# Deviations of sequences 8 to 15 in one batch, the query shift ahead of VectorE's extra work, and column sums of the second weight in step 14

## The reference

```python
x = x + tanh(g_xattn[0]) * xattn(layernorm(x), ctx, ctx, Wq, Wk, Wv, Wo)
x = x + tanh(g_ffn[0]) * ffn(layernorm(x), w1, conv_w, conv_b, w2)

def xattn(q, k, v, ...):            # 16 heads of 16 features
    probs = softmax((q @ Wq.T) @ (k @ Wk.T).T / sqrt(16))
    return (probs @ (v @ Wv.T)) @ Wo.T

def ffn(x, w1, conv_w, conv_b, w2): # 256 -> 1024 -> 256
    h = act_quant(x) @ weight_quant(w1).T     # 8 bit by token, ternary by weight
    h = silu(depthwise_conv1d(h, conv_w, conv_b))   # 3 taps along the sequence
    return act_quant(h) @ weight_quant(w2).T
```

## Time and profile before

| | |
|---|---|
| median of 3 runs | 218.56 us (218.4 to 218.66) |
| the profiled execution | 218.36 us, of which 216.6 are its span |
| busy share of the span | TensorE 92%, its weight loads 75%, VectorE 83%, ScalarE 73%, GpSimd 68% |
| chain of work that ended last | GpSimd 42%, issue 22%, TensorE 18%, VectorE 12% |
| granted TensorE clock, mean | 0.992 of full speed |

### The profile page before, as it was taken

One profiled execution on the slowest core, in us unless ns is written; L12 is line 12 of the kernel. 1 busy time (PEld: TensorE's weight loads), 2 busy tenths in 40 slices (PEclk: granted clock), 3 DMA queues, 4 the chain that ended last, 5 costly groups with the idle time before them and its releaser, 6 DMA issues.

```text
span 216.6 us, 6146 instructions
## 1 busy us (share of the span) xinstructions
PE 199.2 (92%) x2267; PEld 162.9 (75%) x2267; DVE 179.2 (83%) x384; ACT 157.9 (73%) x273; POOL 147.2 (68%) x219
## 2 busy tenths in 40 slices
PE   6999899999989999999979999999989939899995
PEld 6988778788777878788767878877758717687784
DVE  4358686988989898898969889898899979998982
ACT  2347575685866879898878989987989936876541
POOL 2630411853527567988898698898878898999971
PEclk9999999999999999999999999999999988999999
DMA  5999101113022120212210210000002223546543
GB/s 159 338 354 319 51 26 52 47 50 79 20 69 53 38 86 16 73 27 62 53 36 16 55 33 17 2 12 3 3 0 48 51 48 94 101 102 166 116 133 122
DMA packets 29120, 16.95 MB, mean 78 GB/s; under 512 B 17546, under 2 KB 28834, under 8 KB 29090
## 3 DMA queue, kind: packets, MB, share of 16 engines
q1 hardware_dynamic: 29090, 16.55, 28.1%
HBM read 10.50 MB, written 2.11 MB: 58 GB/s over the span
## 4 chain that ended last, share of the span: by engine, by line
POOL 42%; issue 22%; PE 18%; DVE 12%; ACT 2%; DMA 1%; POOLq 1%; DVEq 0%; ACTq 0%
POOL y L489 10%; POOL hid L470 4%; POOL xT L433 4%; POOL xT L435 4%; POOL w2f L477 4%; POOL rstd L442 3%; POOL xn L454 3%; PE ps_av L572 3%; POOL var L439 3%; PE ps_score L657 2%; POOL xq L462 2%; DVE zmax L1438 2%; DVE y L1310 2%; PE ps_proj L623 2%; PE ps_max L667 2%
## 5 line engine op out<-in xcount | busy, mean ns | idle before, releaser
L1253 DVE TENSOR_REDUCE smax<-ps_max 128x8 f32<-128x1024 f32 x31 | 37.8, 1221 | 15.0 <-PE ps_max L667 12.6
L1010 ACT ACTIVATE prob<-ps_score 128x1024 f32<-128x1024 f32 x32 | 32.7, 1020 | 11.5 <-PE ps_score L657 10.6
L657 PE MATMUL ps_score<-Qs,KT 32*128 32x128 f32 x512 | 37.1, 282 | 2.6 <-DVE Qs L1261 1.4
L489 POOL TENSOR_TENSOR y<-y,tap 128x508 f32<-128x508 f32 x30 | 38.6, 1289 | 0.9 <-DVE y L1310 0.6
L657 PEld LDWEIGHTS ps_score<-Qs,KT 32*128 32x128 f32 x512 | 31.2, 186 | 10.0 <-issue 3.7
L667 PE MATMUL ps_max<-KT,QT 32*128 32x256 f32 x248 | 35.1, 400 | 0.0
L454 POOL TENSOR_SCALAR xn<-xn,qa 128x256 f32<-128x256 f32 x16 | 8.6, 536 | 23.2 <-DVE qa L1293 23.1
L1310 DVE SCALAR_TENSOR_TENSOR y<-hid,conv,y 128x508 f32<-128x508 f32 x24 | 23.3, 973 | 0.8 <-ACT y L1048 0.8
L667 PEld LDWEIGHTS ps_max<-KT,QT 32*128 32x128 f32 x248 | 21.1, 184 | 0.1
L477 POOL TENSOR_SCALAR w2f<-y,zmax 128x1024 f16<-128x1024 f32 x16 | 18.0, 1122 | 2.3 <-DVE zmax L1443 1.0
L1438 DVE TENSOR_REDUCE zmax<-y 128x1 f32<-128x1024 f32 x16 | 19.3, 1207 | 0.0
(11 more groups left out here) (145 smaller groups left out, 500.2 us busy)
## 6 DMA issues: line engine op xcount, KB each, us to landing
cin<-ctxT SPq DMA_DIRECT2D x16, 128.0 KB, 3.1
xres<-x SPq DMA_DIRECT2D x16, 128.0 KB, 5.5
out<-xres SPq DMA_DIRECT2D x16, 128.0 KB, 2.0
xT<-xT SPq DMA_DIRECT2D x12, 128.0 KB, 2.3
norm_bc<-norm_dram SPq DMA_DIRECT2D x12, 128.0 KB, 3.2
w1f<-w1T SPq DMA_DIRECT2D x1, 1024.0 KB, 7.3
w2f<-w2T SPq DMA_DIRECT2D x1, 1024.0 KB, 8.7
wk<-wkT SPq DMA_DIRECT2D x1, 256.0 KB, 2.8
```

The lines of the kernel that those rows point to most:

```text
L489: gp.tensor_tensor(y3[:, :, 0:P - 1], y3[:, :, 0:P - 1], tap_buffer(T), ALU.add).then_inc(conv_gp, 1)
L657: mm = pe.matmul(ps_score[:, i * 512 + j * P:i * 512 + (j + 1) * P], KT[b % 3][rows, j * P:(j + 1) * P], Qs[rows, j * P:(j + 1) * P], star ...
L1010: act.activation(prob[pair][:, :], ps_score[:, :], ACT.Exp, scale=DH ** -0.5).then_inc(exp_done, 1)
L1253: dve.tensor_reduce(dst, first_max(n, pair)[:, :].rearrange("p (g t e k) -> p g t e k", g=PG, t=KD, e=2), AX.X, ALU.max).then_inc(max_done, 1)
```

## The change

The statistics of sequences 12 to 15 are taken in step 2 as well, so that GpSimd makes the deviations of sequences 8 to 15 in one batch of eight; the batch of sequences 14 and 15 with its rows, its write and its step is gone. On VectorE shift_q moves ahead of the first slot for extra work, in all steps. The column sums and their copy move from step 7 to step 14, into the PSUM of the values (`ps_v`), in place of the matrices that kept TensorE busy; the first transposes of the last group of quantised inputs now wait for that copy.

```diff
-SUMS_STEP = SB + 3
...
-ROWS = {2: (4, 8), 4: (8, 14), 11: (14, 16)}
+ROWS = {2: (4, 8), 4: (8, 16)}
...
-        ps_w2sum = ps_h[:, 0:D]
+        ps_w2sum = ps_v
...
                 if n == 8:
-                    write_rows(8, 14, 2)
-                if n == 15:
-                    write_rows(14, NB, 3)
-                    load_rows(14, 3)
+                    write_rows(8, NB, 2)
                 turn_xq(n - 6)
-                if n != 14:
-                    load_rows(n, 2 if n < 14 else 3)
+                load_rows(n, 2)
...
                 if s == 2:
-                    norm_rows(8, 14, 4)
-                if s == 9:
-                    norm_rows(14, NB, 5)
+                    norm_rows(8, NB, 4)
...
                 if d >= LAST:

-                    pe.wait_ge(v_done, NB)
+                    pe.wait_ge(sum2_done, 1)
...
-                if d == SUMS_STEP - 3:
-                    pe.wait_ge(sum2_done, 1)
...
-                pe.wait_ge(xq_done, 2 * SB)
-                pe.wait_ge(raw_done, gp_tiles(TILES[SUMS_STEP][0]))
-                pe.wait_ge(scaled_dve, dve_tiles(TILES[SUMS_STEP][0]))
+                pe.wait_ge(k_done, NB)
+                pe.wait_ge(v_done, NB)
...
-                if s == SUMS_STEP:
-                    w2_column_sums()
-                elif seq(d - 1):
+                if seq(d - 1):
                     int_transpose(d - 1, min(tiles, default=0))
                 if seq(n):
                     project_q(n)
-                if s == SUMS_STEP:
-                    int_transpose(d - 1, min(tiles))
...
                 if seq(n + 1):
                     project_k(n + 1)
                 else:
-                    pe.wait_ge(v_done, NB)
-                    keep_busy(4, ps_k)
+                    w2_column_sums()
...
-                if s == SUMS_STEP:
-                    w2_sums_copy()
...
                     k_copy(n + 1)
+                else:
+                    w2_sums_copy()
...
+                shift_q(b)
                 extra(0)
-                shift_q(b)
...
                 if k == 0:
-                    stats_of(10, 11)
+                    stats_of(10, 11, 12)
                 else:
                     weight_scale(0)
-                    stats_of(12, 13)
+                    stats_of(13, 14, 15)
...
-            step(SB + 3, lambda k: stats_of(14) if k == 1 else None)
-            step(SB + 4, lambda k: stats_of(15) if k == 1 else None)
-            for s in range(SB + 5, NB - 1):
+            for s in range(SB + 3, NB - 1):
                 step(s)
```

## The result

The changed kernel takes 215.89 us (median of 4 runs, 215.48 to 216.37) against 218.55 for the kernel before on the same chip (4 runs, 218.4 to 218.66): ratio 0.9881, 95% interval 0.9869 to 0.9894, 2.66 us faster.

The account below looks back on a forecast made before the run. TensorE bounds an ordinary step at a pace of 9.1 us, GpSimd close behind. The terms -0.1 (steps 2 to 6), -0.2 (step 7), -1.3 (step 10) and -0.45 (step 11) sum to -2.05: forecast 216.5 us, range 215.3 to 217.9.

Parts of the forecast that it names:

- Steps 10 and 11: End of the batch: both steps fall to the 9.1 pace without the small batch and its rows, gaining 1.3 and 0.45.
- Column sums: Moved from step 7 to 14: only 0.2 of TensorE's 1.03 arrives; bounds 0 and 1.03.
- Rival 1: Column sums' whole 1.03 arrives, as step 7's GpSimd chain moves forward with an earlier row_max: 215.7; chance 0.12.
- The start of the batch: Steps 1 to 3: two more sequences on VectorE and GpSimd's eight-wide norm_rows cost 0.5, bounds 0.3 and 0.9.
- both delays meet: VectorE's 0.3 and GpSimd's 0.53 meet at the same row stage, so the later counts: 0.5, not their sum.
- The power's 0.53 for two more elements: GpSimd's norm_rows at the batch's start: 1.60 for six is 0.27 each, so two more cost 0.53.
- The shift: Steps 3 to 6, shift_q ahead of extra work: 0.6 gained, limited by VectorE's 0.65 idle in step 5; bounds 0, 1.2.
- go into the lateness above: Step 3: the 0.53 wait for Qs goes into the lateness from the batch's start, not counted as shift gain.
- Rival 4: Normalise behind the weight passes makes TensorE about 0.6 late in each of steps 3 to 6: slower, 219.5; chance 0.10.
- Contention: GpSimd's norm2 power, 0.80 beside weight passes in step 4 and 0.58 in step 3, may take 0.2 more in step 3.
- In step 3 ScalarE's wait for GpSimd: Sign named for the batch's start: a longer wait than the 1.46 ScalarE already stood for norm2's result.
- Everything from step 12 on: Every engine starts the same work earlier by the same amount, so the gain of 2.05 carries to the end.

Follow-up runs that it names:

- the kernels that each removed one of them: Changed kernel with two of step 2's deviations ahead of shift_q: 215.79 us; changed kernel with GpSimd's batch behind norm2 of step 3: 215.86 us.
- the shift alone: Kernel before with only shift_q moved ahead of VectorE's extra work: 217.31 us against 218.58, ratio 0.9937.
- batch alone: Kernel before with only the deviations of sequences 8 to 15 made in one batch: 217.67 us against 218.58, ratio 0.995.
- two deviations ahead and the batch moved: Changed kernel with two deviations ahead of shift_q in step 2 and GpSimd's batch behind norm2 of step 3: 215.58 us against 218.51, ratio 0.9867.
- the last piece apart: Changed kernel with the second weight's last piece split, one pass in step 6, one each ending steps 7 and 9: 215.67 us against 218.51, ratio 0.987.

## Why the prediction was right, and where its sum was off

**Steps 10 and 11** were right in size and mechanism: 1.77 measured for 1.75, ScalarE's wait for GpSimd in step 10 down from 1.71 to 0.31, no wait of project_q in step 11.

**Column sums**: 0.2 forecast; 0.07 to 0.23 by the marks and 0.18 by the times beside the batch, about 0.35 alone. The reason held as well: raw sets step 7. Rival 1's 215.7 lies nearer to the measured 215.89 than the forecast's 216.5, and it is false; only the kernels without the other parts could show that.

**The start of the batch**: 0.5 forecast, 0.42 measured with the shift. That both delays meet and only the later one counts was right, and the kernels that each removed one of them show it: neither gained, both together gained 0.49. Against the shift without a batch (58.81), VectorE's delay alone costs 0.36, where 0.3 was forecast. The power's 0.53 for two more elements was wrong: it divided the whole instruction by six. Where no weight pass runs beside it, the power takes 1.05 for four elements, 1.36 for six (the shift alone) and 1.67 for eight, 0.16 for each further one, 0.31 for two. That 0.5 was met all the same is in part luck. From the batch's first instruction to norm2's shift GpSimd takes 0.42 longer after (4.06) than with the shift alone (3.64): 0.31 is the power, and 0.13 is the first instruction of norm2, which now lies beside a pass (0.41 in place of 0.28).

**The shift** is the mis-sized term: 0.6 forecast with an upper bound of 1.2, measured 1.17 alone and 1.51 beside the batch. Step 5 gave 0.72, near the 0.65 of VectorE's idle time that the prediction set as its limit. What failed is the sentence on step 3, where the 0.53 for Qs "go into the lateness above". The row of step 3 had the same signs as step 5's, a wait for Qs and 0.65 of VectorE idle, and gave 0.39 by itself. Beside the batch the wait it removed had grown to 1.10, so a later VectorE raised the worth of the shift. Shift alone and batch alone add to -1.17 + 0.76 = -0.41 at the mark of step 6; together they give -0.75, and of the 0.34 between them 0.33 stand in step 3 (0.72 against 0.39).

**Rival 4** named a wait that came true: after the change TensorE stood 0.45 in step 3 and 0.27 in step 5 for att. It did not cost 0.6 a step: TensorE's wait for Qs, 0.53 and 0.91, went at the same time, and the steps came out shorter.

**Contention.** norm2's power in step 3 took 0.79 in place of 0.58, as forecast, and in step 4 0.58 in place of 0.80, which nets to nothing. (The 0.58 before ran from 42.81 to 43.39, behind the end of shift_q and so beside normalise, not beside shift_q.) The forecast left out that the same move clears the batch's power: eight elements took 1.90 and 1.89 in the two kernels with the batch but without the shift, and 1.67 with it. GpSimd's timeline of the batch alone, step 3:

```profile
40.21 1.90 POOL L412 TENSOR_TENSOR norm_row<-var,minus_half 128x8 f32<-128x8 f32 x1
```

VectorE's passes start at 41.61 there, so they lie beside its last 0.50; before, they lay beside 0.96 of the power for six, which took 1.60 in place of 1.36. The loss is 0.23 and 0.24 for 0.50 and 0.96 of overlap, and 0.12 for 0.26 with two deviations ahead and the batch moved (1.79). The Trainium skill ("SBUF — State Buffer", "Who interferes with whom") says of GpSimd and a VectorE instruction in a two-port mode, one that takes the ports that both share, that whichever issues first has the shared ports for its whole instruction and blocks the other. The runs agree that the power is slowed by a pass, not that it stands for as long as the pass lasts; whether the passes run in such a mode no run shows.

**Small things.** In step 3 ScalarE's wait for GpSimd rose only from 1.46 to 1.51. Everything from step 12 on moved as a block to within some 0.2. That the stretch behind step 14 agrees to 0.02 is luck: it is 69.26 and 69.24 here and 69.2 to 69.7 in the kernels of the experiments. The 0.21 of steps 12 to 14 is no gain, as it is not there by the second row_max: after step 7, steps of 9.00 to 9.01 alternate with 9.16 to 9.24 by the mark in both kernels, in a different order. What sets this alternation was not tried.

## What to carry to other kernels

When a reordering lets a shared result go first, price every step in which the same pair of signs stands (the consumer waits, the producer later idles), also the steps which another edit delays: the delay makes the reordering worth more. When a delay runs over two engines that meet again, moving the work on one may gain nothing; here the one alone lost 0.26, the other won 0.06, and both together won 0.49. And a total that fits a rival is no evidence for it: take the part out and look at its own step.

## What the runs showed of the hardware that was not expected

VectorE's first tap takes 0.71 to 0.74 by itself and up to 1.83 beside GpSimd's addition; both read two operands from SBUF. The addition keeps its 1.27 in the pair below, but not everywhere: at 96.31 of the same kernel, 0.15 behind the start of a first tap, it takes 1.72. The Trainium skill (the same section as above) says that a VectorE instruction with two SBUF inputs contends with a GpSimd instruction that reads SBUF, and these rows agree. The kernel with the last piece apart, step 7, on VectorE's timeline and on GpSimd's:

```profile
75.93 0.72 DVE L1295 SCALAR_TENSOR_TENSOR y<-hid,conv,y 128x508 f32<-128x508 f32 x1
...
77.68 1.83 DVE L1295 SCALAR_TENSOR_TENSOR y<-hid,conv,y 128x508 f32<-128x508 f32 x1
```

```profile
77.48 0.27 POOL L439 TENSOR_SCALAR shift<-mv,rstd 128x1 f32<-128x1 f32 x1
77.70 1.27 POOL L484 TENSOR_TENSOR y<-y,tap 128x508 f32<-128x508 f32 x1
```

In the other direction GpSimd's shift of 128x1 takes 0.27 here and 0.73 to 1.05 where a first tap, or a pass and a tap, lie beside it. In every such pair of these runs the shift ends 0.04 to 0.15 behind the tap's end, so this instruction does stand for as long as VectorE's lasts, unlike the power above. In step 8 of this kernel the tap starts at 87.18, ahead of the shift at 87.31, and the shift takes 0.74; in the changed kernel it starts at 87.81, behind the shift at 87.50, and the shift takes 0.27 and the tap 1.72. ScalarE then stands 0.73 for the shift in steps 8 and 10, and the second hidden tile 0.33 for raw: this is how these steps gave back part of what step 7 won. That the passes at the ends of steps 7 and 9 are what brought the tap ahead of the shift was not tested apart.
